# Expert stage of a mixture-of-experts block: the PE transposes of gathered rows replaced by a transposing DMA of 16-bit halves

## Chip, cores and metric

One NeuronCore of one Trainium2 chip runs the whole program in one launch. The metric is the device time of an execution in microseconds, lower is better.

## What is computed

The input x has 4096 rows of 256 float32. The block is `x += 0.5 * moe(norm(x))`, `x += attention(norm(x))`, `x += 0.5 * moe(norm(x))`. The mixture of experts, with 32 experts, 6 of them chosen for each row, is

```
scores = sigmoid(xf @ gate.T)                       # 4096 x 32
topk   = top_k(group-masked(scores + bias), 6)
tw     = 2.5 * scores[topk] / sum(scores[topk])
g, u   = xf @ gate_up[e][:128].T, xf @ gate_up[e][128:].T
routed = sum over chosen e of  tw_e * (silu(g) * u) @ down[e].T
out    = routed + shared expert(xf)
```

The attention part (a local one over segments of 64 rows and a global one over the segments' means) isn't touched by the change.

## The kernel before

The program runs six stages after one another: routing of the first mixture, its experts, the sum of the answers, attention with the routing of the second mixture beside it, the second mixture's experts, and the combining that writes the output.

**Routing.** For each pair of 128-row tiles, VectorE finds the six experts of every row, its six weights and six places. `act_route_rows` (L1227) copies the two normalised tiles on ScalarE (L1232, 128 partitions x 512 float32) into `rows`, whose rows are 320 floats long: 256 of data, 32 weights and 32 destinations, one for each expert. GpSimd scatters each row to its six places in the HBM tensor `dispatch_rows` by an indirect DMA (L632, L656).

**Experts.** The rows of an expert lie together in `dispatch_rows`, and are taken in blocks of 128: NB = 224 blocks for each of the two mixtures, so 448 turns in all. A table `itab` in SBUF holds each block's expert and first row; an engine's sequencer reads a number of it into a register (TENSOR_LOAD in the trace). A turn of block n is spread over the engines, each of which works through an order fixed by hand:

- SyncE (`sp_experts`): reads the block's first row from the table (L510) and issues the load of 128 x 320 floats into one of 4 buffers (L515).
- TensorE (`pe_experts`): transposes block n+2 into PSUM by two 128x128 products (`tx`, L831), multiplies block n by the staged gate and up weights (L711, 8 instructions of `xbt,ans`), and block n-2 by the down weights (L711, 2 instructions of `wdn,hb`).
- ScalarE (`act_experts`): silu of block n into `sg` (L1280), the copy of the gate and up weights of block n+2 from `wgu` into `staged` (L1274, recorded as `ans<-wgu`), the copy of the transposed block n+2 from PSUM to `xbt` (`xt_copy`, L1266), and the reading of one table entry, the expert of block n+3 (L1285).
- VectorE (`v_experts`): the product `hb` (L1714), the answer scaled by the row's weight (`yb`/`ans`, L1724), the scatter list `didx` (L1721), and two picks for each block (L1703): of the 32 weights and the 32 destinations in a row, the one that belongs to the block's expert.
- GpSimd (`pool_experts`): the indirect DMA that scatters the answers (L672), with 8 answer buffers.

TensorE waits for `staged` and `xt` of the block, ScalarE's silu waits for TensorE's `gu`, and the staging copy of block n+2 waits for `gu` of block n, whose buffer it takes.

Of the kernel before, what the change touches and what calls it, by code (L numbers as in the profile page):

```python
# [9 lines left out]
U32 = mybir.dt.uint32  # L10
ALU = mybir.AluOpType
# [26 lines left out]
COL_W, COL_DEST = D, D + E  # L38
# [71 lines left out]
def build(nc, x_in, gate_t, gate_bias, wgu_in, wdn_in, wsg_in, wsu_in, wsd_in,  # L110
          wi_l, bi_l, wo_l, bo_l, wi_g, bi_g, wo_g, bo_g, out):
    ctx = ExitStack()
    with ctx:
# [83 lines left out]
        rows = blk  # L197
        xbt = sb("xbt", [P, 2, D])
# [3 lines left out]
        picked = sb("picked", [P, 2, E])  # L202
        wcol = sb("wcol", [P, 8])
        dcol = sb("dcol", [P, 8])
        didx = sb("didx", [P, 8], I32)
# [40 lines left out]
        more_rows = flat[:, E * E + 4 * P:E * E + 4 * P + 4 * ROW].rearrange("p (q r) -> p q r", q=4)  # L246
        more_answers = flat[:, 0:4 * D].rearrange("p (q d) -> p q d", q=4)

        def block_rows(q):
            return blk[:, q, :] if q < 4 else more_rows[:, q - 4, :]  # L250
# [101 lines left out]
        LOADS, ANSWERS = 4, 8  # L352

        row_loads = [sem(f"ex_ld{q}") for q in range(LOADS)]

        class ExpertSems:
            def __init__(self, n):
# [5 lines left out]
                self.ld = row_loads  # L363
                self.loaded_by_now = n * 16 * (NB // LOADS)
                self.tx = s("ex_tx")
                self.xt = s("ex_xt")
# [132 lines left out]
        def sp_experts(sp, r, s):  # L499

            sp.wait_ge(s.tab, 1)
            for q in range(4):
                sp.wait_ge(r.scat[q], 16 * TOPK * (NT // 4))
            sp.wait_ge(padded, 16 * E)
            sp.wait_ge(ld_small, N_SMALL)

            def body(g, peeled):
                for q in range(LOADS):
                    n = g * LOADS + q
                    first = sp.value_load(itab[0:1, bass.ds(n + 2 * P, 1)], min_val=0, max_val=E * CAP - P)  # L510

                    if not peeled:
# [3 lines left out]
            body(0, True)  # L516
            with sp.Fori(1, NB // LOADS) as g:
                body(g, False)

        def sp_sum(sp, x, s):  # L520
            ans_v = answers_dram.rearrange("(n p k) d -> n p (k d)", p=P, k=TOPK)

            for q in range(ANSWERS):
                sp.wait_ge(x.scat[q], 16 * (NB // ANSWERS))
            for i in range(NT):
# [20 lines left out]
        def sp_combine(sp, x, s):  # L546
# [20 lines left out]
            for i in range(NT):  # L567
                load_answers(i)
                p = i // 2
                if i == 1:  # L570

                    sp.wait_ge(x.tx, NB)
                    sp.wait_ge(x.pick, 2 * NB)
# [42 lines left out]
        def pool_route_fours(pool, s):  # L616

            def pair(p, q0):
# [3 lines left out]
                for m in range(2 * TOPK):  # L623
# [4 lines left out]
                    if m == 8 and pair_exists(p + 1):  # L628
# [4 lines left out]
                        out=rows_dram, out_offset=bass.IndirectOffsetOnAxis(ap=idx[:, q, k:k + 1], axis=0),  # L633
                        in_=rows[:, q, :], in_offset=None).then_inc(s.scat[q], 16)
            pairs_by_two(pool, lambda p, k: pair(p, 2 * k), NT // 2)

        def pool_route_paced(pool, s):
# [5 lines left out]
            def pair(p, q0):  # L643
# [3 lines left out]
                for t in range(2):  # L647
                    i = p * 2 + (6 + t)
                    for k in range(TOPK):
                        if exists(i):  # L650
# [6 lines left out]
                            out=rows_dram, out_offset=bass.IndirectOffsetOnAxis(ap=idx[:, q, k:k + 1], axis=0),  # L657
                            in_=rows[:, q, :], in_offset=None).then_inc(s.scat[q], 16)
# [7 lines left out]
        def pool_experts(pool, s):  # L666
            with pool.Fori(0, NB // ANSWERS) as g:
                for q in range(ANSWERS):

                    pool.wait_ge(s.y, g * ANSWERS + (q + 1))  # L670
# [3 lines left out]
                        in_=block_answers(q), in_offset=None, bounds_check=T * TOPK - 1,  # L674
                        oob_is_err=False).then_inc(s.scat[q], 16)
# [136 lines left out]
        TX, GU, DN = 0, 2, 6  # L812
# [7 lines left out]
        def pe_experts(pe, s):  # L820
# [5 lines left out]
            def tx(n, q):  # L826

                b = q % LOADS
                pe.wait_ge(s.ld[b], loaded(s, n, b))
                for c in range(KC):  # L830
                    m = pe.transpose(ps[:, TX + q % 2, c * P:(c + 1) * P], block_rows(b)[:, c * P:(c + 1) * P], ident[:])  # L831
                m.then_inc(s.tx, 1)

            def step(n, q, m=None):
                j = q % 2
                if m is None or n < NB:
                    pe.wait_ge(s.staged, n + 1)
                    pe.wait_ge(s.xt, n + 1)  # L840

                    for half in range(2):
                        for c in range(KC):
                            g = mm(ps[:, GU + q % 4, half * P:(half + 1) * P],
                                   staged[:, j, c, half * I:(half + 1) * I],
                                   xbt[:, j, c * P:(c + 1) * P], start=(c == 0), stop=(c == KC - 1))
                    g.then_inc(s.gu, 1)
                if m is None or n >= 2:
                    e = pe.snap(expert[j], min_val=0, max_val=E - 1)
                    pe.wait_ge(s.h, n - 1)  # L850
                    positive(pe, s.y, n - 3)
                    mm(ps[:, DN + j, 0:D], hb[:, j, :], wdn[:, bass.ds(e * D, D)]).then_inc(s.d, 1)
                if m is None or n + 2 < NB:
                    tx(n + 2, (q + 2) % 8)
# [4 lines left out]
            tx(0, 0)  # L859
            tx(1, 1)  # L860
# [366 lines left out]
        def act_route_rows(act, s, p, k):  # L1227
# [4 lines left out]
            act.copy(rows[:, 2 * k:2 * k + 2, 0:D], xn[:, 2 * k:2 * k + 2, :]).then_inc(s.rx, 1)  # L1232
# [29 lines left out]
        def act_experts(act, s):  # L1262
            def xt_copy(n, j):
                act.wait_ge(s.tx, n + 1)
                positive(act, s.gu, n - 1)
                act.copy(xbt[:, j, :], ps[:, TX + j, 0:D]).then_inc(s.xt, 1)  # L1266

# [8 lines left out]
            def step(n, q, m=None):  # L1276
                j = q % 2
                act.wait_ge(s.gu, n + 1)
                positive(act, s.h, n - 1)
                act.activation(sg[:, j, :], ps[:, GU + q, 0:P], ACT.Silu).then_inc(s.sg, 1)  # L1280
# [6 lines left out]
            act.wait_ge(s.tab, 1)  # L1287
            act.wait_ge(ld_exp, 16 * 3 * (NT // 2))
            for j in range(2):
                act.reg_load(expert[j], itab[0:1, j:j + 1])  # L1290
            xt_copy(0, 0)
            stage(0, 0)
            xt_copy(1, 1)
            stage(1, 1)
            act.reg_load(expert[0], itab[0:1, 2:3])
            for n in range(4):
                step(n, n, m=0)
            with act.Fori(1, NB // 4 - 1) as g:
                for q in range(4):
                    step(g * 4 + q, q)  # L1300
            for n in range(NB - 4, NB):
                step(n, n % 4, m=0)
# [388 lines left out]
        def v_experts(v, st, s):  # L1691
            start = st.base + st.n
            st.rebase(start)

            def pick(n, q):

                b = q % LOADS
                v.wait_ge(s.ld[b], loaded(s, n, b))

                positive(v, s.pick, n * 2)  # L1700
                positive(v, s.y, n - 3)
                for k, (col, out_) in enumerate(((COL_W, wcol), (COL_DEST, dcol))):
                    v.scalar_tensor_tensor(  # L1703
                        out=picked[:, k, :], in0=iota_e[:], scalar=etab[:, bass.ds(n, 1)],
                        in1=block_rows(b)[:, col:col + E], op0=ALU.is_equal, op1=ALU.mult,
                        accum_out=out_[:, q:q + 1]).then_inc(s.pick, 1)

            def step(n, q, m=None):
# [6 lines left out]
                if m is None or n >= 2:  # L1715

                    at_, k = (q + 6) % 8, (q + 6) % 8 % ANSWERS
                    per = 16 // ANSWERS
                    positive(v, s.scat[k],
                             16 * ((n - 2) // ANSWERS) if isinstance(n, int) else n * per - (2 + k) * per)  # L1720
# [398 lines left out]
```

## Time and profile before

| | |
|---|---|
| time, median of 3 runs | 1511.45 us (1508.77 to 1520.38) |
| the profiled execution | span 1514.0 us; no separate device time is given for it |
| busy, of the span | PE 1311.2 (87%), DVE 1092.3 (72%), ACT 745.8 (49%), POOL 921.6 (61%) |
| DMA | 275.35 MB, mean 182 GB/s |

### The profile page before, as it was taken

The numbers are of one execution on the slowest core, as the hardware profiler recorded it, in microseconds if no ns is written. First come the engines' busy times: TensorE is split into PE (matmuls) and PEld (weight loads), VectorE is DVE, ScalarE is ACT, GpSimd is POOL, SyncE is SP. The second block draws the span as 40 slices with busy tenths as digits, with TensorE's granted clock in tenths as the row PEclk, the third lists the DMA queues.
The fourth block names the chain that finished last, engine by engine and source line by source line (L and its number), as shares of the span: only waits on it lengthen the run. The fifth ranks groups of instructions, "written<-read, shape, count | busy, mean of one in ns | idle before, by whom it ended". The sixth has DMA issues, their size and how long they took to land.

```text
span 1514.0 us, 50415 instructions
## 1 busy us (share of the span) xinstructions
PE 1311.2 (87%) x10768; PEld 1150.5 (76%) x10769; DVE 1092.3 (72%) x5484; ACT 745.8 (49%) x2296; POOL 921.6 (61%) x981
## 2 busy tenths in 40 slices
PE   6877772799999999789989998952999999999986
PEld 5766661699999999678766766742999999999765
DVE  6676654478888888576368888863788888888576
ACT  3433320466666666300356666721666666666100
POOL 3777777466666666422017776775566666666687
PEclk9776775899999999899699999955999999999998
DMA  9963333465556555397003333444565556564698
GB/s 316 404 248 130 126 130 127 146 184 184 186 185 190 181 187 178 119 330 256 1 29 136 142 131 131 147 174 144 176 188 187 184 183 186 180 184 139 231 315 280
DMA packets 155771, 275.35 MB, mean 182 GB/s; under 512 B 28966, under 2 KB 108091, under 8 KB 155712
## 3 DMA queue, kind: packets, MB, share of 16 engines
q1 hardware_dynamic: 115776, 161.32, 34.6%
q0 software_dynamic: 39936, 113.33, 20.2%
q8 instruction: 26, 0.43, 0.1%
q14 instruction: 33, 0.27, 0.1%
HBM read 147.64 MB, written 135.27 MB: 187 GB/s over the span
## 4 chain that ended last, share of the span: by engine, by line
PE 30%; DVE 7%; DMA 5%; issue 4%; POOL 3%; ACT 1%; DVEq 0%; SPq 0%; POOLq 0%; ACTq 0%
PE ps L711 26%; DMA ans<-answers 4%; PE ps L831 3%; POOL dispatch_rows L656 2%; DVE smax L1926 1%; DVE yb L1846 1%; POOL xres L693 1%; DVE stats L1469 0%; DVE prob L1936 0%; DVE rstd L1456 0%; DVE newt L1454 0%; DVE newt L1455 0%; PE ps L719 0%; DMA blk<-normed_transposed 0%; POOL answers L672 0%
## 5 line engine op out<-in xcount | busy, mean ns | idle before, releaser
L711 PE MATMUL ps<-xbt,ans 128*128 128x128 f32 x3584 | 477.0, 276 | 0.3 <-ACT ans L1274 0.3
L711 PEld LDWEIGHTS ps<-xbt,ans 128*128 128x128 f32 x3584 | 439.0, 193 | 0.9 <-ACT ans L1274 0.8
L672 POOL DMA_INDIRECT answers<-yb,didx x224 | 220.2, 983 | 160.9 <-issue 118.0
L672 POOL DMA_INDIRECT answers<-ans,didx x224 | 220.1, 983 | 122.2 <-issue 120.2
L1703 DVE SCALAR_TENSOR_TENSOR picked<-iota_e,etab,blk 128x32 f32<-128x32 f32 x896 | 190.7, 250 | 119.9 <-DVE yb L1724 40.1
L656 POOL DMA_INDIRECT dispatch_rows<-blk,idx x192 | 188.4, 981 | 142.9 <-issue 129.3
L1274 ACT COPY ans<-wgu 128x512 f32 x448 | 274.6, 613 | 0.2 <-issue 0.2
L711 PE MATMUL ps<-wdn,hb 128*128 x896 | 267.6, 381 | 1.3 <-DVE ans L1724 1.3
L632 POOL DMA_INDIRECT dispatch_rows<-blk,idx x192 | 187.3, 976 | 79.0 <-issue 57.2
L1280 ACT ACTIVATE sg<-ps 128x128 f32<-128x128 f32 x448 | 124.4, 278 | 218.5 <-PE ps L711 216.8
L831 PE MATMUL ps<-ident,blk 128*128 128x128 f32 x896 | 172.9, 275 | 33.6 <-DMA blk<-dispatch_rows 33.6
L1266 ACT COPY xbt<-ps 128x256 f32<-128x256 f32 x448 | 165.6, 370 | 64.6 <-PE ps L831 64.6
L831 PEld LDWEIGHTS ps<-ident,blk 128*128 128x128 f32 x896 | 126.9, 142 | 79.1 <-issue 33.0
L1714 DVE TENSOR_TENSOR hb<-ps,sg 128x128 f32<-128x128 f32 x448 | 130.6, 291 | 54.7 <-PE ps L711 23.6
L711 PEld LDWEIGHTS ps<-wdn,hb 128*128 128x128 f32 x896 | 136.0, 192 | 2.5 <-issue 2.5
L1724 DVE TENSOR_SCALAR ans<-ps,wcol 128x256 f32<-128x256 f32 x224 | 108.0, 482 | 1.1 <-PE ps L711 0.9
L1724 DVE TENSOR_SCALAR yb<-ps,wcol 128x256 f32<-128x256 f32 x224 | 108.3, 483 | 0.0
L1382 ACT ACTIVATE ans<-ps,nmax 128x64 f32<-128x64 f32 x256 | 76.4, 323 | 26.3 <-DVE nmax L1927 26.1
L711 PEld LDWEIGHTS ps<-xnt,wsgu 128*128 128x128 f32 x528 | 72.7, 216 | 2.8
L1703 DVE DVE_READ_ACCUMULATOR picked<-iota_e,etab,blk 128x1 f32 x896 | 74.5, 83 | 0.1
L711 PE MATMUL ps<-wsd,hsh 128*128 128x256 f32 x192 | 72.3, 543 | 2.2 <-DVE hsh L1832 2.2
L1721 DVE TENSOR_TENSOR didx<-dcol,ans 128x1 int32<-128x1 f32 x448 | 72.8, 163 | 0.0
(230 smaller groups left out, 1996.7 us busy)
## 6 DMA issues: line engine op xcount, KB each, us to landing
blk<-dispatch_rows SPq DMA_DIRECT2D x448, 160.0 KB
ans<-answers SPq DMA_DIRECT2D x54, 512.0 KB, 4.9
ans<-answers SPq DMA_DIRECT2D x54, 256.0 KB, 4.8
wgu<-in_gate_up SPq DMA_DIRECT2D x32, 256.0 KB
dispatch_rows<-blk,idx POOLq DMA_INDIRECT x384, 2.5
dispatch_rows<-padt SPq DMA_DIRECT2D x32, 160.0 KB
yb<-answers SPq DMA_DIRECT2D x10, 512.0 KB, 4.8
wdn<-in_down SPq DMA_DIRECT2D x16, 256.0 KB
```

Of the source, the lines that this page charges most:

```text
L632: pool.indirect_dma_start(out=rows_dram, out_offset=bass.IndirectOffsetOnAxis(ap=idx[:, q, k:k + 1], axis=0), in_=rows[:, q, :], in_offset ...
L656: pool.indirect_dma_start(out=rows_dram, out_offset=bass.IndirectOffsetOnAxis(ap=idx[:, q, k:k + 1], axis=0), in_=rows[:, q, :], in_offset ...
L672: pool.indirect_dma_start(out=answers_dram, out_offset=bass.IndirectOffsetOnAxis(ap=didx[:, q:q + 1], axis=0), in_=block_answers(q), in_of ...
L711: return nc.tensor.matmul(out_, lhs, rhs, start=start, stop=stop)
L831: m = pe.transpose(ps[:, TX + q % 2, c * P:(c + 1) * P], block_rows(b)[:, c * P:(c + 1) * P], ident[:])
L1266: act.copy(xbt[:, j, :], ps[:, TX + j, 0:D]).then_inc(s.xt, 1)
L1274: act.copy(staged[:, j, :, :], wgu[:, :, bass.ds(e * (2 * I), 2 * I)]).then_inc(s.staged, 1)
L1280: act.activation(sg[:, j, :], ps[:, GU + q, 0:P], ACT.Silu).then_inc(s.sg, 1)
L1382: a = act.activation(ssub[:, at_, :], ps[:, r, c * SEG:(c + 1) * SEG], ACT.Exp, bias=nmax[:, h:h + 1], scale=float(HDL) ** -0.5, accum_out ...
L1703: v.scalar_tensor_tensor(out=picked[:, k, :], in0=iota_e[:], scalar=etab[:, bass.ds(n, 1)], in1=block_rows(b)[:, col:col + E], op0=ALU.is_ ...
L1714: v.tensor_tensor(hb[:, j, :], ps[:, GU + q % 4, P:2 * P], sg[:, j, :], ALU.mult).then_inc(s.h, 1)
L1724: v.tensor_scalar(block_answers(k), ps[:, DN + j, 0:D], wcol[:, at_:at_ + 1], None, ALU.mult).then_inc(s.y, 1)
```

## The change

Rows are stored differently. In `dispatch_rows` a row of 320 floats becomes two planes of 320 16-bit numbers: the low (or high) halves of the 256 data values and half of the weights and destinations' space, then the other. `act_route_rows` writes this by a copy of 16-bit elements. For each block SyncE issues one transposing DMA, which sees the block as 256 rows (128 rows x 2 planes) of 256 16-bit numbers and writes them turned, so that SBUF holds float32 values, transposed; TensorE uses them as they land. TensorE's transposes and ScalarE's `xt_copy` are dropped. There are 8 such buffers in place of 4. The weights and destinations of a block (128 rows x 2 pieces of 128 bytes) are loaded by a second, plain DMA, which ScalarE issues at the end of the turn of the block eight before, after reading a second table entry. VectorE picks for four blocks at once, by one comparison, one product, one sum and one addition in four consecutive turns. TensorE's down product has four PSUM banks in place of two; the scatter lists have 16 columns in place of 8.

```diff
 # SyncE, for each block
-                    first = sp.value_load(itab[0:1, bass.ds(n + 2 * P, 1)], min_val=0, max_val=E * CAP - P)
-                        sp.wait_ge(s.tx, n - (LOADS - 1))
-                        sp.wait_ge(s.pick, n * 2 - (2 * LOADS - 2))
-                    sp.dma_start(block_rows(q), rows_dram[bass.ds(first, P), :]).then_inc(s.ld[q], 16)
+                    sp.reg_load(first[1 - q % 2], itab[0:1, bass.ds(n + 1 + 2 * P, 1)])
+                block_rows = rows_dram[bass.ds(at_, P), :]
+                positive(sp, s.gu, n - (LOADS - 1))
+                sp.dma_start_transpose(
+                    out=turned_halves(q % LOADS),
+                    in_=block_rows.bitcast(U16).rearrange("r (h x) -> (r h) x", h=2)[:, 0:D]
+                    ).then_inc(s.ld[q % LOADS], 16)
 # TensorE
-                    pe.wait_ge(s.xt, n + 1)
+                    pe.wait_ge(s.ld[q % LOADS], loaded(s, n, q % LOADS))
-                if m is None or n + 2 < NB:
-                    tx(n + 2, (q + 2) % 8)
 # ScalarE, routing
-            act.copy(rows[:, 2 * k:2 * k + 2, 0:D], xn[:, 2 * k:2 * k + 2, :]).then_inc(s.rx, 1)
+            act.copy(planes(rows[:, 2 * k:2 * k + 2, :])[:, :, :, 0:D],
+                     halves(xn[:, 2 * k:2 * k + 2, :])).then_inc(s.rx, 1)
 # ScalarE, experts
+            def load_pairs(n, q, group):
+                at_ = act.snap(first, min_val=0, max_val=E * CAP - P)
+                positive(act, s.pick, group - 1)
+                act.dma_start(pairs_of(q // PICKED % 2)[:, q % PICKED],
+                              rows_dram[bass.ds(at_, P), :].rearrange("r (h x) -> r h x", h=2)[:, :, D // 2:]
+                              ).then_inc(s.pairs[q // PICKED % 2], 16)
+                if not isinstance(n, int) or n + 1 < NB:
+                    act.reg_load(first, itab[0:1, bass.ds(n + 1 + 2 * P, 1)])
                 if m is None or n + 2 < NB:
                     stage(n + 2, j)
-                    xt_copy(n + 2, j)
                 if m is None or n + 3 < NB:
                     act.reg_load(expert[1 - j], itab[0:1, bass.ds(n + 3, 1)])
+                if m is None or n + 8 < NB:
+                    load_pairs(n + 8, q, n // PICKED + 2 if isinstance(n, int) else turn * 2 + q // PICKED + 2)
+            for n in range(8):
+                load_pairs(n, n, n // PICKED)
             act.wait_ge(ld_exp, 16 * 3 * (NT // 2))
 # VectorE, one of these in each turn, for four blocks
+            def mark(n):
+                st.did(v.tensor_tensor(
+                    mine, iota_e[:].unsqueeze(1).to_broadcast([P, PICKED, E]),
+                    etab[:, bass.ds(n, PICKED)].unsqueeze(2).to_broadcast([P, PICKED, E]), ALU.is_equal))
+            def take(k, paired):
+                v.wait_ge(s.pairs[k], paired)
+                v.tensor_tensor(picked, pairs_of(k), mine.unsqueeze(2).to_broadcast([P, PICKED, 2, E]),
+                                ALU.mult).then_inc(s.pick, 1)
+            def reduce_(k, group):
+                st.did(v.tensor_reduce(wd[:, k], picked, X_AXIS, ALU.add))
+            def lists(n, q):
+                st.did(v.tensor_tensor(didx[:, q:q + PICKED], wd[:, k, :, 1], skip[:, bass.ds(n, PICKED)], ALU.add))
```

## Rows read from the trace of the kernel before

**Rows 1.** Windows, one for each stage: busy us (instructions), granted clock, DMA share, GB/s

```profile
0.00:272.00 272.00, 177.86 (x940) 154.72 (x941) 165.26 (x874) 77.41 (x130) 189.53 (x213) 0.74 0.57 209
272.00:623.00 351.00, 347.94 (x2681) 324.83 (x2682) 277.32 (x1561) 237.80 (x671) 215.16 (x219) 0.99 0.58 177
...
1050.00:1403.00 353.00, 349.36 (x2689) 326.27 (x2690) 277.06 (x1567) 239.23 (x673) 215.61 (x220) 0.99 0.57 176
```

**Rows 2.** The chain that ended last: start us, us, what

```profile
1060.04 1.33 PE ps L711 x10
...
1381.57 1.33 PE ps L711 x10
```

**Rows 3.** Timeline of one turn: start us, us, what [idle before <- releaser]

```profile
552.28 0.60 PE L711 MATMUL ps<-wdn,hb 128*128 x2
552.48 0.28 ACT L1280 ACTIVATE sg<-ps 128x128 f32<-128x128 f32 x1 [0.40 <-PE ps L711]
...
552.65 0.61 ACT L1274 COPY ans<-wgu 128x512 f32 x1
...
552.71 0.38 PE L831 MATMUL ps<-ident,blk 128*128 128x128 f32 x2
...
552.93 1.06 PE L711 MATMUL ps<-xbt,ans 128*128 128x128 f32 x8
```

**Rows 4.** Sequencer instructions at three lines, 1060 to 1390 us: ns min/median/max

```profile
L1285 ACTq TENSOR_LOAD <-itab x214: 272/392/585, 1060.1 to 1389.4; - x107
L1285 ACTq FUSED_REGOPS  x212: 42/43/43, 1063.2 to 1389.3; - x106
...
L515 SPq DMA_DIRECT2D blk<-dispatch_rows x213: 332/333/408, 1061.4 to 1389.3; - x107
...
L510 SPq FUSED_REGOPS  x373: 46/152/159, 1060.4 to 1389.7; - x187
L510 SPq TENSOR_LOAD <-itab x214: 262/268/413, 1060.1 to 1389.8; - x107
```

**Rows 5.** Timeline of SyncE's queue: issues at the program's start and of the first blocks

```profile
1.30 0.50 SPq L448 DMA_DIRECT2D wgate<-in_gate  x1
...
4.91 8.75 SPq L459 DMA_DIRECT2D wil<-in_wi_local  x1
...
272.11 1.46 SPq L515 DMA_DIRECT2D blk<-dispatch_rows  x2
...
274.33 1.42 SPq L515 DMA_DIRECT2D blk<-dispatch_rows  x2
```

**Rows 6.** Timeline of the start of the first expert stage

```profile
275.30 0.62 ACT L1274 COPY ans<-wgu 128x512 f32 x1
```

**Rows 7.** Groups on DVE and ACT, 1060 to 1390 us: busy us, mean ns | idle before

```profile
L1703 DVE SCALAR_TENSOR_TENSOR picked<-iota_e,etab,blk 128x32 f32<-128x32 f32 x426 | 90.4, 250 | 45.0 <-DVE ans L1724 22.6 <-DVE yb L1724 20.2 <-issue 0.5
L1714 DVE TENSOR_TENSOR hb<-ps,sg 128x128 f32<-128x128 f32 x214 | 62.3, 291 | 20.5 <-PE ps L711 9.7 <-ACT sg L1280 0.3
L1724 DVE TENSOR_SCALAR yb<-ps,wcol 128x256 f32<-128x256 f32 x108 | 52.2, 483 | 0.0
...
L1266 ACT COPY xbt<-ps 128x256 f32<-128x256 f32 x214 | 79.1, 370 | 0.0
```

**Rows 8.** Timeline, GpSimd's shortest distances

```profile
67.34 0.96 POOL L632 DMA_INDIRECT dispatch_rows<-blk,idx  x1 [0.30 <-DVE yb L1484]
68.61 0.96 POOL L632 DMA_INDIRECT dispatch_rows<-blk,idx  x1 [0.30 <-issue]
...
1402.65 0.98 POOL L672 DMA_INDIRECT answers<-yb,didx  x1 [3.14 <-DVE ans L1724]
1403.94 0.98 POOL L672 DMA_INDIRECT answers<-ans,didx  x1 [0.30 <-DVE ans L1724]
```

**Rows 9.** The row copy, its line over the whole run: ns min/median/max

```profile
L1232 ACT COPY blk<-yb x32: 609/619/623, 11.8 to 1022.9; 128x512 f32<-128x512 f32 x32
```

**Rows 10.** DMA queues: packets, MB, share of 16 engines' span

```profile
q1 hardware_dynamic: 115776, 161.32, 34.6%
q0 software_dynamic: 39936, 113.33, 20.2%
```

**Rows 11.** Windows around a fall of the clock in the attention stage, columns as in rows 1

```profile
780.00:870.00 90.00, 81.73 (x1252) 62.63 (x1251) 75.94 (x361) 60.71 (x275) 58.01 (x60) 1.00 0.35 125
870.50:877.30 6.80, 5.24 (x102) 3.73 (x100) 5.73 (x26) 4.59 (x23) 4.61 (x6) 1.00 0.33 121
877.40:880.70 3.30, 3.30 (x8) 2.64 (x9) 2.52 (x13) 2.12 (x13) 2.39 (x4) 0.50 0.30 110
```

More of the change, by code:

```diff
@@ L10 @@
 U32 = mybir.dt.uint32
+U16 = mybir.dt.uint16
 ALU = mybir.AluOpType
@@ L197, in build, with planes, halves @@
         rows = blk
+        def planes(tiles):
+            return tiles.bitcast(U16).rearrange("p q (h x) -> p q h x", h=2)
+        def halves(tiles):
+            return tiles.bitcast(U16).rearrange("p q (d h) -> p q h d", h=2)
         xbt = sb("xbt", [P, 2, D])
@@ L349, in __init__ @@
                     self.sh_x = s("sh_x")
-        LOADS, ANSWERS = 4, 8
+        LOADS, ANSWERS, PICKED, LISTS = 8, 8, 4, 16
         row_loads = [sem(f"ex_ld{q}") for q in range(LOADS)]
+        pair_loads = [sem(f"ex_pairs{k}") for k in range(2)]
         class ExpertSems:
@@ L666, in pool_experts @@
         def pool_experts(pool, s):
-            with pool.Fori(0, NB // ANSWERS) as g:
-                for q in range(ANSWERS):
-                    pool.wait_ge(s.y, g * ANSWERS + (q + 1))
+            with pool.Fori(0, NB // LISTS) as g:
+                for q in range(LISTS):
+                    pool.wait_ge(s.y, g * LISTS + (q + 1))
                     pool.sem_inc(s.take, 1)
@@ L1260, in act_route, with act_experts @@
             pairs_by_two(act, body, NT // 2)
[L1262 to L1266, printed above, removed]
+        def act_experts(act, r, s):
             expert = [act.alloc_register(f"staged_expert{j}_{s.n}") for j in range(2)]
@@ L1290, in act_experts @@
                 act.reg_load(expert[j], itab[0:1, j:j + 1])
-            xt_copy(0, 0)
             stage(0, 0)
-            xt_copy(1, 1)
             stage(1, 1)
             act.reg_load(expert[0], itab[0:1, 2:3])
[L1296 to L1302, printed above, removed]
+            for n in range(8):
+                step(n, n, None, m=0)
+            with act.Fori(1, NB // 8 - 1) as g:
+                for q in range(8):
+                    step(g * 8 + q, q, g)
+            for n in range(NB - 8, NB):
+                step(n, n % 8, None, m=0)
         def act_combine(act, s):
@@ L1722, in step @@
-                    v.wait_ge(s.d, n - 1)
-                    v.wait_ge(s.pick, n * 2 - 2)
-                    v.tensor_scalar(block_answers(k), ps[:, DN + j, 0:D], wcol[:, at_:at_ + 1], None, ALU.mult).then_inc(s.y, 1)
-                    st.sync()
-                if m is None or n + 2 < NB:
-                    pick(n + 2, (q + 2) % 8)
-            pick(0, 0)
-            pick(1, 1)
-            for n in range(16):
-                step(n, n % 8, m=0)
-            with v.Fori(2, NB // 8 - 1) as g:
-                for q in range(8):
-                    st.rebase(g * 8 + (start + q - 2))
-                    step(g * 8 + q, q)
@@ L1737, in v_experts @@
-            st.rebase(start + NB - 8 - 2)
-            for n in range(NB - 8, NB + 2):
-                step(n, n % 8, m=0)
+                             16 * ((n - 2) // ANSWERS) if isinstance(n, int) else turn * 32 + 16 * ((q - 2) // ANSWERS))
+                    st.sync()
+                    v.tensor_scalar(block_answers(k), ps[:, DN + b % 4, 0:D], wd[:, b // PICKED % 2, b % PICKED, 0:1],
+                                    None, ALU.mult).then_inc(s.y, 1)
+                phase, group = q % PICKED, q // PICKED + 1
@@ new lines, in step @@
+                if m is None or n // PICKED * PICKED + PICKED < NB:
+                    if phase == 0:
+                        mark(n + PICKED)
+                    elif phase == 1:
+                        take(group % 2, s.paired_by_now + 64 * (group // 2 + 1) + (
+                            n // LISTS * 128 if isinstance(n, int) else turn * 128))
+                    elif phase == 2:
+                        reduce_(group % 2, n // PICKED + 1 if isinstance(n, int) else turn * 4 + group)
+                    else:
+                        lists(n + 1, (q + 1) % LISTS)
@@ new lines, in v_experts @@
+            mark(0)
+            take(0, s.paired_by_now + 64)
+            reduce_(0, 0)
+            lists(0, 0)
+            for n in range(LISTS):
+                step(n, n, None, m=0)
+            base_n = st.base + st.n
+            with v.Fori(1, NB // LISTS - 1) as g:
+                st.rebase(g * 12 + (base_n - 12))
+                for q in range(LISTS):
+                    step(g * LISTS + q, q, g)
+                assert st.n == 12, st.n
+            st.rebase(base_n + (NB // LISTS - 2) * 12)
@@ L1741, in v_sum @@
+            for n in range(NB - LISTS, NB + 2):
+                step(n, n % LISTS, None, m=0)
         def v_sum(v, st, s):
```

119 lines of the change are left out of this document (61 added, 58 removed).

## The prediction

> **What bounds the kernel.** I read the windows by stage first. In both expert stages TensorE is busy for all but 3 or 4 us (347.94 of 351.00, 349.36 of 353.00) at a granted clock of 0.99, that is the 2.4 GHz level, while ScalarE, VectorE and GpSimd stand at 238, 277 and 215 us [rows 1]. The chain of waits says the same in its own way: it runs through TensorE alone. Pieces of ten products (L711) of 1.33 us return from 1060.04 to 1381.57, which is 208 turns of 1.546 us [rows 2]; the 0.216 that is left of each turn is the two transposes (L831), and the timeline of a turn shows just that, 552.71 to 552.93 [rows 3]. So the stage is bound by TensorE's work, 448 turns of 1.546 us = 693 us of the 1514.0 us of the profiled execution. No device time of its own is given for that execution; its span is 2.6 us above the median 1511.45, and I add what changes to the median.
>
> **What TensorE gives up.** 448 x 0.216 = 97 us. That would be the gain if nothing else came late: 1.33 us a turn.
>
> **What ScalarE takes on.** Its busy time hides it. It gives up the 0.370 us copy (L1266) [rows 7], and the silu and the staging copy, 0.28 + 0.61, fill only 0.89 of a turn [rows 3]. But its sequencer works in order and carries out table reads and DMA issues itself, while its engine works off what was handed over. So I add up the sequencer's turn, from silu to silu, with 0.045 us between one sequencer instruction and the next. That distance I work out from SyncE: two issues span 1.46 or 1.42 us, so a turn of it is 1.09 to 1.12 [rows 5]; its durations are a table read 0.268, a check of 0.152, an issue of 0.333 [rows 4] and some 0.09 of small register operations (two like L1285's 0.043), 0.84 together, and the rest lies in six gaps.
> 1. Silu to staging copy: 0.17 (552.48 to 552.65) [rows 3]; then 0.05 to the next instruction.
> 2. Its own table read for the expert, already there today: 0.043 + 0.392 + two gaps = 0.52 [rows 4].
> 3. New, before the issue: a register move, a wait with its operand, the address; three times 0.035 to 0.045 plus gaps = 0.25.
> 4. New: the issue. SyncE's of one piece for each partition takes 0.333 [rows 4]; the load of `wgate`, 128 partitions x 2 pieces of 128 bytes and so of the very shape of the new one, took 0.50 [rows 5]. With gap 0.38 to 0.55. ScalarE issues no DMA before, so both are SyncE's prices. I take the lower, since the issues of one-piece loads at the program's start were dearer than those in the stage, too.
> 5. New: the second table read, 0.043 + 0.392 + two gaps = 0.52.
> 6. The two waits ahead of the next silu: 0.14; the step over the loop's end, shared by eight turns, 0.03 at most.
>
> The sum is 0.22 + 0.52 + 0.25 + 0.38 + 0.52 + 0.14 = 2.03; part of the small operations overlap with the gaps in my count, and the table reads vary from 0.272 to 0.585 [rows 4], so with reads of 0.272 it is 1.79. The low end, with gaps of 0.035 as well, is 1.72; the high end, with 0.50 for the issue, is 2.16. I take 1.96, nearer the row of the median read than that of the shortest. None of it waits for TensorE, so nothing hides it once TensorE's own turn is 1.33: silu of n+1 and the staging of n+3 queue behind it, and TensorE waits for `staged`. What covered ScalarE until now was its wait of 0.40 for TensorE in each turn [rows 3]; the cover is smaller than what is added (1.15 us added, about 0.15 given up with `xt_copy`). Turns with the new load: 432 of 448 (the last eight of each stage have none and gain 0.21 each). 432 x (1.96 - 1.546) = +179, less 3 = **+176 us**.
>
> The Trainium skill, "DMA: Bandwidth & Descriptors", section "Issuing engines are not separate DMA queues", says that starting DMAs from several engines saves only the sequencer's time for initiating them, which is usually small beside the DMA. By that rule the new issue would cost nothing, and it points to the first rival below. The rows of this case speak against "small": 0.333 to 0.50 us in a turn of 1.546.
>
> **The start of each expert stage.** ScalarE now issues eight loads before its first staging copy, and waits for the last scatter first. It starts where SyncE starts, at 272.1 [rows 5]. Eight times SyncE's turn without its check, 0.93, or with the dearer issue and reads 1.2, is 7.4 to 9.6; two reads follow, 0.8. The first staging copy moves from 275.30 [rows 6] to about 281.5. Nothing hides it, TensorE has no other work. Twice +6 = **+12 us**. The transposed blocks land in that time.
>
> **The row copy.** L1232 takes 0.619 us for 512 elements [rows 9]. With 16-bit halves there are 1024. From 256 elements at 0.370 [rows 7] to 512 at 0.619 each costs 0.97 ns, so it takes 1.12, +0.50 for each of 32 pairs. In the first routing GpSimd sets the pace (189.53 us busy in scatters 1.27 apart [rows 1, 8]), and the copy is done a pair ahead: nothing. In the attention stage 16 of them are beside busy engines; between 0 and 8 us, I take **+5**. If 16-bit elements went faster it would be at most 0.6 x 16 = 10 less; nothing here shows that.
>
> **VectorE.** It gives up two picks (2 x 0.25 and more than 0.1 behind them) and a list of 0.16 in each turn, and does one of four: a comparison of 128 elements, at most 0.29 like `hb`, a product of 256 and a sum of 256, 0.48 each like the answer [rows 7], an addition. With `hb` and the answer a turn is at most 0.29 + 0.48 + 0.48 = 1.25 us, below 1.33. It ends nothing.
>
> **GpSimd.** Its shortest distances are 1.27 and 1.29 us [rows 8]: below 1.33. It is 0.04 from being the next bound, and free here.
>
> **SyncE.** It no longer has the check, but a DMA whose kind no row shows: read, operations and gaps come to 0.6, so at a turn of 1.96 the issue may take 1.3 us unnoticed, at 1.33 only 0.7. From below: a plain issue, 0.333. From above: an issue held by a full queue took 8.75 [rows 5]. I take it as hidden, nearest to the plain issue by size (128 KB against 160).
>
> Sum: 1511.45 + 176 + 12 + 5 = **1705 us**. Its own range, from turns of 1.72 to 2.16 us, is 1600 to 1795. Chance 0.53.
>
> **Rivals.**
>
> *TensorE stays the bound (faster).* If the issue is handed on at once and the second read overlaps, ScalarE's turn falls below 1.33 and the stage runs at TensorE's pace: 1511.45 - 97 + 12 + 5 = about 1432, with GpSimd's 1.29 right behind. For it: ScalarE's engine is idle a third of the turn. Against it: on SyncE issue, read and next issue follow one another without overlap. It decides if the sequencer's turn is under 1.33, against my 1.72 at the least. Chance 0.17. In between, a turn of 1.48 to 1.54, lies no change: 0.06.
>
> *The transposing DMA sets the pace (slower still).* Packets of SyncE's queue take 0.346 x 16 x 1514 / 115776 = 72 ns, those of GpSimd's 0.202 x 16 x 1514 / 39936 = 123 ns [rows 10]. A turn loads 128 and scatters some 32 now: 0.58 + 0.25 us of 16 engines. If the 256 half rows go as 256 packets at 72 ns the turn needs 1.15 + 0.25 + up to 1.15 for the small pieces; as 512 packets, 2.3 + 0.25 and more, some 2.6. It decides from 1.96 on, and at 2.6 gives 1511 + 448 x 1.05 + 17 = 2000. Chance 0.15. The Trainium skill has two figures, in sentences that the sum does without. "DMA: Bandwidth & Descriptors", section "Latency and other measured facts", gives a transposing DMA 261 GB/s: an estimate of 0.50 us for 131 KB, no bound. "VectorE: DVE Perf Modes", section "The three transpose paths", gives 1309 ns for 128 x 128 in 16 bits; a block is four of them, by an estimate 5.2 us if they followed one another, and the time would be over 3000. No row here shows either.
>
> *TensorE's clock falls.* With 1.33 us of work in 1.96, TensorE has a gap in every turn. In the attention stage the clock stayed at 1.00 with TensorE busy for 81.73 of 90.00 us, and fell to 0.50 (1.2 GHz) after a stretch with 5.24 of 6.80, which is 77%; 3.4 us later it was back [rows 11]. At that level a turn's work takes 2.66. If 3.4 of every 10.2 us went so, they would hold 3.4/2.66 + 6.8/1.96 = 4.75 blocks, 2.15 us for one: +82, 1787 us. Chance 0.09.
>
> **From cases to numbers.** Faster by over 1%: the first rival, 0.17. Within 1%, about what a measurement of this kernel can tell from no change: 0.06. Slower by over 1%: 0.53 + 0.15 + 0.09 = 0.77. To leave out no more than 2 in 10 the range must reach from the faster rival to above the clock's: 1430 to 1850; the likeliest case's own range is 1600 to 1795.
>
> **What the changed profile would show.** If I am right: ScalarE's sequencer without waits in the stage, silu to silu in 1.7 to 2.15 us, TensorE idle before its L711 for `staged` (the copy `ans<-wgu`), its busy share in the stage near 70 to 80%, the first staging copy some 6 us later. If TensorE's gaps end with the landing of the turned rows, it is the transposing DMA; if granted clock is 0.5 in stretches, the third rival; if L711 pieces follow at 1.33, the first. The prediction fails above all if ScalarE's issue or reads cost half of what I assume.

## The result and the profile after

The changed kernel takes 1737.21 us, median of 4 runs (1733.9 to 1743.72), against 1510.92 for the kernel before; the ratio is 1.1502, interval 1.1471 to 1.1533. The prediction was 1705, with 1600 to 1795 for its likeliest case.

The windows of the profiled execution (span 1742.0 us), cut at the same events as in [rows 1]:

```profile
0.00:270.20 270.20, 175.49 (x940) 151.93 (x941) 165.57 (x875) 84.20 (x130) 189.26 (x213) 0.72 0.58 210
270.20:735.00 464.80, 357.43 (x2248) 270.96 (x2248) 206.52 (x677) 178.56 (x452) 218.36 (x222) 0.98 0.61 133
...
1169.00:1630.00 461.00, 357.56 (x2251) 271.22 (x2252) 205.26 (x671) 178.07 (x449) 216.86 (x221) 0.98 0.61 135
```

Nearly all of the loss lies in the two expert stages: 925.8 us against 704, of a span that grew by 228. TensorE was busy for 99% of them before; now it is for 77%, and no other engine is busier: by busy time nobody bounds the stage. The chain of waits of the page names what busy time leaves out:

```profile
PE 14%; ACTq 12%; issue 8%; DVE 5%; ACT 5%; DMA 4%; POOL 2%; DVEq 0%; SPq 0%; POOLq 0%
PE ps L738 13%; ACTq L1293 5%; ACTq L1297 4%; ACT ans L1286 3%; DMA ans<-answers 3%; ACTq L1307 2%; POOL dispatch_rows L683 1%; DMA blk<-normed_transposed 1%; DVE smax L1973 1%; DMA dispatch_rows<-blk,idx 1%; DVE yb L1893 1%; ACT ans L1393 0%; ACTq L1286 0%; DVE stats L1497 0%; ACT sg L1303 0%
```

ACTq is ScalarE's sequencer: the issue of the small load (L1293), the read of its first row (L1297), the read of the expert (L1307). Before, ACTq stood at 0%. The waits from 300 to 700 us say who waits in consequence (engine, line <- releaser: us in total, times, longest):

```profile
DVE hb L1750 <- ACT sg L1303: 191.1, 168, 1.9
...
ACT sg L1303 <- PE ps L738: 113.4, 79, 1.8
...
PE ps L738 <- ACT ans L1286: 89.2, 195, 1.0
```

TensorE waits for the staging copy once in each of some 200 turns, and not once in this list for the turned rows. The middle line says that the silu waited for TensorE 79 times. That is only the event that came last before the silu; what ScalarE did meanwhile is read from its sequencer, below.

The turn itself, from the line of the silu (first and last start of each stage):

```profile
L1303 ACT ACTIVATE sg<-ps x224: 271/277/278, 282.2 to 729.3; 128x128 f32<-128x128 f32 x112
...
L1303 ACT ACTIVATE sg<-ps x224: 269/277/279, 1181.2 to 1626.3; 128x128 f32<-128x128 f32 x112
```

(729.3 - 282.2)/223 = 2.005 us and 1.996 us, against 1.546 of [rows 2]. What fills it, by the sequencers' lines, 300 to 700 us (ns min/median/max):

```profile
L1297 ACTq TENSOR_LOAD <-itab x196: 274/382/780, 300.0 to 698.7; - x196
...
L1307 ACTq TENSOR_LOAD <-itab x196: 271/278/312, 300.8 to 699.4; - x196
...
L1293 ACTq DMA_DIRECT2D blk<-dispatch_rows x98: 550/551/588, 301.3 to 695.8; - x98
...
L534 SPq DMA_TRANSPOSE blk<-dispatch_rows x100: 1186/1189/1362, 299.9 to 693.3; - x100
...
L530 SPq TENSOR_LOAD <-itab x198: 263/329/607, 301.2 to 698.7; - x198
```

ScalarE: 0.28 + 0.38 for the reads, 0.55 for the issue, the rest small operations and gaps. But SyncE has a long turn too: the transposing issue holds its sequencer for 1.19 us (the plain issue of [rows 4] 0.33), and with a read of 0.33 and the rest a turn of SyncE's own would be some 1.8 to 1.9.

The lines above don't tell two engines with turns so near each other apart. The distances between one sequencer instruction and the next, added up, do; between two that don't wait it is 0.03 to 0.05 us. From 300 to 700 us ScalarE's sequencer stands still for more than 0.13 us only 25 times, 5.6 us in all, of which 5.3 lie at the end of its loop: it doesn't wait, whatever the list of waits names. SyncE's stands still 82 times, 25.8 us in all, each time ahead of an issue, where it waits for a buffer to come free. So SyncE follows, with 0.13 us of slack in a turn. The experiments test this.

### The profile page after: what moved, and what is told of

Same layout as the page of the kernel before. It is cut to its first block, busy times and chain, and to the rows that moved or that the text cites. A ratio compares the mean times of both kernels' runs of the same rounds, so it can differ in the third digit from the quotient of the medians.

```text
span 1742.0 us, 44022 instructions
## 1 busy us (share of the span) xinstructions
PE 1332.0 (76%) x9872; PEld 1041.7 (60%) x9873; DVE 948.2 (54%) x3692; ACT 636.6 (37%) x1848; POOL 923.2 (53%) x981
## 3 DMA queue, kind: packets, MB, share of 16 engines
q1 hardware_dynamic: 294976, 146.67, 31.0%
## 4 chain that ended last, share of the span: by engine, by line
PE 14%; ACTq 12%; issue 8%; DVE 5%; ACT 5%; DMA 4%; POOL 2%; DVEq 0%; SPq 0%; POOLq 0%
PE ps L738 13%; ACTq L1293 5%; ACTq L1297 4%; ACT ans L1286 3%; DMA ans<-answers 3%; ACTq L1307 2%; POOL dispatch_rows L683 1%; DMA blk<-normed_transposed 1%; DVE smax L1973 1%; DMA dispatch_rows<-blk,idx 1%; DVE yb L1893 1%; ACT ans L1393 0%; ACTq L1286 0%; DVE stats L1497 0%; ACT sg L1303 0%
## 5 line engine op out<-in xcount | busy, mean ns | idle before, releaser
L738 PE MATMUL ps<-blk,ans 128*128 128x128 f32 x1792 | 261.1, 290 | 149.2 <-ACT ans L1286 149.0
L738 PEld LDWEIGHTS ps<-blk,ans 128*128 128x128 f32 x1792 | 220.9, 194 | 234.8 <-issue 230.5
L738 PE MATMUL ps<-kt,ans 128*128 128x128 f32 x896 | 128.8, 287 | 44.2 <-ACT ans L1286 44.1
L738 PE MATMUL ps<-prob,ans 128*128 128x128 f32 x896 | 128.6, 286 | 43.1 <-ACT ans L1286 42.9
L738 PEld LDWEIGHTS ps<-kt,ans 128*128 128x128 f32 x896 | 108.7, 191 | 87.1 <-issue 84.1
L738 PEld LDWEIGHTS ps<-prob,ans 128*128 128x128 f32 x896 | 108.9, 191 | 85.4 <-issue 84.1
L1758 DVE TENSOR_SCALAR ans<-ps,wd 128x256 f32<-128x256 f32 x224 | 106.3, 476 | 0.3 <-PE ps L738 0.2
L1758 DVE TENSOR_SCALAR yb<-ps,wd 128x256 f32<-128x256 f32 x224 | 106.3, 474 | 0.0
L738 PE MATMUL ps<-xnt,wsgu 128*128 128x128 f32 (+1 forms) x528 | 68.8, 292 | 0.0
L746 PE MATMUL ps<-ident,yb 128*128 128x128 f32 x128 | 30.6, 328 | 42.2 <-DVE yb L1512 38.7
```

What stands on the lines that cost most here:

```text
L738: return nc.tensor.matmul(out_, lhs, rhs, start=start, stop=stop)
L1758: v.tensor_scalar(block_answers(k), ps[:, DN + b % 4, 0:D], wd[:, b // PICKED % 2, b % PICKED, 0:1], None, ALU.mult).then_inc(s.y, 1)
```

## Experiments

Theory 1: ScalarE's sequencer sets the turn of 2.00. Theory 2: SyncE's transposing issue does. Theory 3: the DMA engines or the landing do.

On two of the chips used, the kernel before itself took 1909 and 1881 us. ScalarE and VectorE stop there now and then for several us, for up to 20.3 in the routing, and the profile names nothing of this program as the releaser ("remote"). Kernels whose sequencers were relieved (below) still had turns of 2.10 and 2.05 us on them, so something else sets the pace there. I call these chips disturbed, and compare each run only with kernels on a chip of the same kind.

### Twice the same read: an edit that wasn't there

```diff
+                    act.reg_load(first, itab[0:1, bass.ds(n + 1 + 2 * P, 1)])   # ScalarE, doubled
+                    sp.reg_load(first[1 - q % 2], itab[0:1, bass.ds(n + 1 + 2 * P, 1)])   # SyncE, in the other kernel
```

> The changed kernel with the second table read of ScalarE's turn (the first row for the small load) done twice; results are the same. Theory 1, ScalarE's sequencer sets the turn of 2.00 us: every turn grows by a read and its address, 0.35 to 0.50 us, so +150 to +215 on 1737, about 1910. Theory 2, SyncE's transposing issue (1.19 us, with its read and waits some 1.9) sets it and ScalarE has only followed: ScalarE's slack would take most of it, under +60. Theory 3, the DMA engines or the landing of the turned rows set it: no change.

> The changed kernel with SyncE's table read done twice; results are the same. Theory 1: SyncE's own turn is 1.85 to 1.93 us against ScalarE's 2.00, so of the 0.35 to 0.40 us added some 0.1 is hidden: a turn of 2.2 to 2.3, +100 to +130. Theory 2: nothing is hidden, +155 to +180. Theory 3: under +20, since buffers are loaded eight blocks ahead.

> The same kernel as act_extra_read, beside a kernel before of some 1515. If ScalarE's sequencer sets the turn of 2.00 us (theory 1), each of its turns grows by 0.35 to 0.50: a turn of 2.35 to 2.5, 1890 to 1960. If SyncE at 1.82 to 1.93 set it with ScalarE only following (theory 2), ScalarE at its own 1.85 to 2.0 plus the read would still pass it, but by less: under +100 on 1737. If the DMA engines set it (theory 3), no change.

Measured: 1895.85 and 1895.76 us on a chip where the kernel before takes 1908.95 (ratios 0.989 and 0.994); the third, on an ordinary chip, 1739.88 against 1511.73, ratio 1.150 [1.145, 1.156], as the changed kernel. The pages show why: all three runs have 44022 instructions, exactly as many as the changed kernel. The doubled read isn't in any of the three; since its result is overwritten by the next, it was most likely dropped as dead. So these say nothing on any theory; they are three more runs of the changed kernel. They give two useful things: its time repeats, and on a chip of the disturbed kind it takes 1896 with a turn of (813.6 - 364.8)/223 = 2.01.

### A read that is used

```diff
-                act.copy(staged[:, j, :, :], wgu[:, :, bass.ds(e * (2 * I), 2 * I)])
+                act.copy(staged[:, j, :, :], wgu[:, :, bass.ds(e * I + e2 * I, 2 * I)])
+                    act.reg_load(again[1 - j], itab[0:1, bass.ds(n + 3, 1)])
```

> The changed kernel with a third table read in ScalarE's turn, of the block's expert again into another register, and both registers in the staging copy's address, so that no read can be dropped as dead (act_extra_read had as many instructions, 44022, as the changed kernel: its doubled read wasn't there). Results are the same. ScalarE's sequencer as the bound: 0.28 to 0.45 for the read, 0.1 to 0.15 for its operations, a turn of 2.4 to 2.6, so 1910 to 2010. If ScalarE had slack: under +50 on 1737.

Measured: 2021.64 us on a disturbed chip (the kernel before: 1881.22; ratio 1.0762 [1.0711, 1.0812]), where the changed kernel had 1895.85 on the other of that kind. The new read and the silu:

```profile
L1310 ACTq TENSOR_LOAD <-itab x171: 274/276/574, 400.3 to 797.9; - x171
```

```profile
L1305 ACT ACTIVATE sg<-ps x224: 277/278/278, 356.7 to 872.3; 128x128 f32<-128x128 f32 x112
```

The turn is (872.3 - 356.7)/223 = 2.31, 0.30 more than 2.01; 448 x 0.30 = 134, and the times differ by 126. Both are under what I expected of theory 1 (a turn of 2.4 to 2.6, 173 to 273 us more) and over the 50 us that slack would have left. The new read takes 0.276 us, and its gap and operations come on top, but the read of the first row became shorter at the same time, from a median of 0.377 us in act_extra_read to 0.280. The two chips aren't the same one, which is this run's weak point; its own trace makes up for it. From 400 to 800 us ScalarE's sequencer stands still for over 0.13 us for 5.4 us in all, nearly all of it at the end of its loop, and SyncE's for 94.2. So the turn of 2.31 is what ScalarE's sequencer needs. That is theory 1.

### SyncE relieved

A plain load of the same bytes takes the place of the transposing one, so the experts' inputs aren't transposed, and the routing's row copy moves 512 float32.

```diff
-                sp.dma_start_transpose(
-                    out=turned_halves(q % LOADS),
-                    in_=block_rows.bitcast(U16).rearrange("r (h x) -> (r h) x", h=2)[:, 0:D]
+                sp.dma_start(
+                    turned_rows(q % LOADS).rearrange("p (h x) -> p h x", h=2),
+                    block_rows.rearrange("r (h x) -> r h x", h=2)[:, :, 0:D // 2]
```

> SyncE issues a plain load of the same 128 KB (two pieces of 512 bytes a row) in place of the transposing DMA, and the row copy of the routing moves 512 float32 in place of 1024 16-bit halves. The experts' inputs then aren't transposed, all other work is done. SyncE's issue should fall from 1.19 to about 0.5 us. Theory 1: ScalarE's sequencer still sets the turn, 1.8 to 2.0, so 1650 to 1730; if its reads were lengthened by SyncE's issues, it is the lower end. Theory 2 and 3: the turn falls to TensorE's 1.33 to 1.5, 1440 to 1510. The attention stage with the routing shows what the dearer row copy costs: 0 to 14 us less than in the changed kernel.

> The same kernel as plain_in_place_of_transposing (experts' inputs not transposed, a plain load of the same bytes, a row copy of 512 float32), beside a kernel before of some 1515. Theory 1: ScalarE alone holds the turn at 1.8 to 2.0, 1640 to 1735. Theory 2 or 3: SyncE or the DMA engines are relieved and the turn falls toward 1.33 to 1.5. In the attention stage the cheaper row copy gives back 0 to 14 us.

Measured: 1896.23 on the disturbed chip (before: 1908.95, ratio 0.992), which can't tell them apart; on an ordinary one 1718.83 against 1511.73, ratio 1.137 [1.132, 1.142].

```profile
L1303 ACT ACTIVATE sg<-ps x224: 270/277/279, 283.3 to 726.2; 128x128 f32<-128x128 f32 x112
```

```profile
L534 SPq DMA_DIRECT2D blk<-dispatch_rows x98: 542/543/544, 299.7 to 690.6; - x98
```

SyncE's issue fell from 1.19 to 0.54 us, and the turn from 2.00 to (726.2 - 283.3)/223 = 1.99. SyncE's sequencer now stands still for 162.2 us of 400, ScalarE's for 5.6 as before. Theories 2 and 3 fall: neither SyncE nor the transposing in the DMA engines held the turn of the changed kernel. Against act_extra_read_2 on the same chip the time fell by 21 us: some 7 are the turns, and 10 lie between the two expert stages, where two profiles of the changed kernel differ by as much (see the row copy, below).

### ScalarE relieved

One table read in every eighth turn fills eight registers.

```diff
-                    act.reg_load(expert[1 - j], itab[0:1, bass.ds(n + 3, 1)])
-                    act.reg_load(first, itab[0:1, bass.ds(n + 1 + 2 * P, 1)])
+                    if q == 6:
+                        act.reg_load(expert, itab[0:1, bass.ds(n + 2, 8)])
+                    if q == 0:
+                        act.reg_load(first, itab[0:1, bass.ds(n + 8 + 2 * P, 8)])
```

> ScalarE reads eight experts and eight first rows by one table read each in every eighth turn, into eight registers, in place of two reads in each turn; results are the same. Theory 1: ScalarE's turn falls by 0.28 + 0.41 + operations, some 0.75, to 1.3, and SyncE becomes the bound at 1.85 to 1.93: 1670 to 1705. Theory 2: the same end, so only by how little it gains do they differ (theory 2: nothing). Theory 3: no change. If neither SyncE nor DMA held it, TensorE's 1.33 would give about 1440.

> The same kernel as scalar_reads_batched, again, since in that call the kernel before itself took 1909 us and every variant landed beside it: scatters there paused for 3 to 4 us at a time, also in the routing. Beside a kernel before of some 1510: theory 1 (ScalarE's sequencer sets the turn of 2.00 us) expects ScalarE's own turn to fall to about 1.1 and SyncE's, 1.85 to 1.93, to take over: 1670 to 1705. Theory 2 (SyncE's transposing issue set it all along): under 20 us gained. Theory 3 (DMA engines or landing): no change.

Measured: first 1923.83 on the disturbed chip (before: 1908.95, ratio 1.008), with a turn of (832.0 - 364.7)/223 = 2.10, no answer; then 1656.46 against 1517.25, ratio 1.0929 [1.0885, 1.0972]. The turn is (687.6 - 282.1)/223 = 1.82:

```profile
L1302 ACT ACTIVATE sg<-ps x224: 277/278/278, 282.1 to 687.6; 128x128 f32<-128x128 f32 x112
```

and TensorE's weight loads now wait for another:

```profile
ACT sg L1302 <- PE ps L738: 190.0, 199, 2.3
...
PEld ps L738 <- DMA blk<-dispatch_rows: 70.1, 89, 2.0
```

Taking two reads of ScalarE's away gave 81 us; adding one cost 126. The difference between removing and adding is SyncE, which stood 0.18 us behind ScalarE and became the bound: its sequencer doesn't once stand still for over 0.13 us from 300 to 680 us, while ScalarE's does for 117 us. The time is below my 1670 to 1705, since SyncE's read takes a median of 0.268 us now and took 0.329 in the changed kernel.

### Both relieved, with and without the transposing

```diff
-                    sp.reg_load(first[1 - q % 2], itab[0:1, bass.ds(n + 1 + 2 * P, 1)])
+                if q % 8 == 0:
+                    sp.reg_load(first, itab[0:1, bass.ds(n + 2 * P, 8)])
```

> As before, and SyncE too reads eight first rows at once in every eighth turn; results are the same. SyncE's turn becomes the issue of 1.19 us, some 0.2 of operations and gaps, and an eighth of a read of 0.55: 1.45 to 1.5. Theories 1 and 2 both expect that turn, so 1480 to 1530, near the kernel before; if theory 3 holds (the turned rows cost the DMA engines more than the issue shows) it stays above 1600. TensorE's own 1.33 is not reached.

> Plain load in place of the transposing DMA (experts' inputs not transposed) and both engines' table reads batched by eight. ScalarE's turn is 1.1, SyncE's 0.8, so TensorE at 1.33 or GpSimd at 1.29 to 1.33 sets it: 1511 - 97 + 10 = 1420 to 1440, the price of the prediction's first rival. If it stays above 1480, the DMA engines (by 16-bit halves or by small pieces) or a wait that no theory has are the bound.

Measured: with the transposing DMA 1534.22 against 1517.25, ratio 1.0127 [1.0084, 1.017], just above my 1480 to 1530; with the plain load 1449.86 against 1511.73, ratio 0.9563 [0.9505, 0.962], above my 1420 to 1440. Silu lines and the windows 300 to 570 us, with transposing:

```profile
L1301 ACT ACTIVATE sg<-ps x224: 277/278/278, 282.2 to 630.6; 128x128 f32<-128x128 f32 x112
```

```profile
300.00:570.00 270.00, 247.88 (x1712) 209.31 (x1711) 157.59 (x513) 136.63 (x342) 169.24 (x173) 1.00 0.91 181
```

and with the plain load:

```profile
L1301 ACT ACTIVATE sg<-ps x224: 277/277/279, 280.3 to 588.2; 128x128 f32<-128x128 f32 x112
```

```profile
300.00:570.00 270.00, 268.51 (x1955) 244.62 (x1955) 178.79 (x585) 156.09 (x390) 192.92 (x196) 1.00 0.79 207
```

Turns of 1.56 and 1.38 us. Plain, TensorE is busy for 268.51 of 270 again: the rival that the prediction priced at 1432 exists, once both sequencers are out of the way, and costs 1450. With the transposing issue it can't be reached. The DMA engines are busy for 0.91 of the stage, against 0.79 plain at a faster turn, so both they and SyncE could hold the last 0.18 us. TensorE waits for the turned rows in this kernel:

```profile
PEld ps L737 <- DMA blk<-dispatch_rows: 32.4, 47, 1.4
```

SyncE's sequencer is the nearer cause: from 300 to 600 us it stands still for over 0.13 us for 7.7 us in all, 4.5 of them at the end of its loop, so it hardly waits for a free buffer and issues as fast as it can. What fills its turn of 1.56 is the issue, 1.22 us in the mean, an eighth of a table read of eight (below), and small operations with their gaps:

```profile
L529 SPq TENSOR_LOAD <-itab x23: 521/543/808, 310.4 to 589.8; - x23
```

The DMA engines' part is at most that the issue grows longer as they are busier: its mean is 1.19 us at a share of 0.53 (the kernel with the used read), 1.20 at 0.63, 1.22 at 0.91. Why it does isn't shown.

### Toward a version that beats both

```diff
+            stage(0, 0)
+            stage(1, 1)                       # ScalarE: now ahead of the wait for the last scatter
             for q in range(4):
                 act.wait_ge(r.scat[q], 16 * TOPK * (NT // 4))
-                    sp.reg_load(first, itab[0:1, bass.ds(n + 2 * P, 8)])
+                    sp.reg_load(first, itab[0:1, bass.ds(n + 2 * P, 16)])
```

> On both_reads_batched (1534): ScalarE stages its first two weights before it waits for the last scatter and issues its eight loads, and SyncE reads 16 first rows at once in a loop of 16 blocks; results are the same. The first takes 3 to 5 us from each stage's start, the second some 1.0 us from every 16 turns, 14 a stage: -28 us if SyncE sets the turn. 1495 to 1515 if so; if the DMA engines, busy for 0.89 of the stage there, set it, 1520 to 1530.

> On early_staging_reads_of_16 (1522.6), SyncE reads 32 first rows at once in a loop of 32 blocks; results are the same. If SyncE's sequencer sets the turn, some 1.0 us less from every 32 turns, so -10 to -14: 1508 to 1513, the time of the kernel before. If the DMA engines set it, busy for 0.93 of the stage there: no gain, 1518 to 1525.

Measured: with 16, 1522.6 against 1511.73, ratio 1.0046 [1.0016, 1.0077], a turn of (621.7 - 278.2)/223 = 1.54 with the DMA engines at 0.93; with 32, 1879.87 against 1881.22 on a disturbed chip, ratio 0.9979 [0.9955, 1.0004], which doesn't tell whether 32 gains over 16.

The 1522.6 falls into the range that I had put down to the DMA engines, but the trace doesn't say so: SyncE's sequencer never stands still for over 0.13 us from 300 to 600 us. I had priced the gain wrongly. A read of 16 costs nearly what two of eight do, where I had expected 1.0 us from every 16 turns, and the mean issue rose from 1.22 to 1.24 us:

```profile
L529 SPq TENSOR_LOAD <-itab x12: 837/1102/1192, 320.5 to 593.4; - x12
```

No transposing version beats the kernel before. The silu of the first block starts at 278.2, against 282.2: that is the cost of the eight issues ahead of the staging copy.

## Why the prediction was right

**TensorE's work and the gain it would give.** Right that a gain waited behind the sequencers, but 97 us isn't what the runs show of it: the plain kernel with batched reads had a turn of 1.38 and not 1.33, as its ten products for a block fill 1.37 us (268.51 us for 1955 products). That is 0.166 us less than 1.546, or 74 us in 448 turns, and the time was 62 us less than before.

**ScalarE's sequencer.** The step that decided, and right as a mechanism: predicted 1.96 us, measured 2.00. Its trace shows no waits, as the prediction said it would, and three runs carry it: with a used read the turn grows and ScalarE's sequencer stays full, relieving SyncE changes the turn by 0.01, relieving ScalarE lowers it to SyncE's.

How near the number came is in part luck, since mis-sized terms cancelled. The issue takes 0.551 us, where I took 0.333 and named 0.50 from the row of `wgate` as the upper price: the load of the same shape, not the nearest in time, was the right row. ScalarE's own read, carried over at 0.392, takes 0.278 now; the new one has 0.382. Together +0.22, -0.11 and -0.01 make +0.10 us on the sum of 2.03. The turn came out 0.03 below that sum, so its small operations and gaps were 0.13 too dear. That I took 1.96 and not the sum of 2.03 was a judgement for the shorter reads, and no run shows it as such. By its own terms the high end of the turn was 2.20 (2.03 - 0.333 + 0.50) and not 2.16; the measured 2.00 is inside both.

Why the one read takes 0.28 us and the other 0.38 isn't shown. The dearer one coincides with a table read of TensorE's (L875) in 195 of 196 turns, the cheaper one never; but in the kernel with the used read 21 that coincide have a median of 0.279.

The Trainium skill says that issuing is usually small beside the DMA ("DMA: Bandwidth & Descriptors", section "Issuing engines are not separate DMA queues"). In plain_in_place_of_transposing_2 the small load of 32 KB lands a median of 2.4 us after its issue, so 0.551 us is about a quarter of it. What decided here is another comparison: 0.551 us of a turn of 2.00.

The 0.04 us by which 1.96 was missed are, over 432 turns, 17 us of the 32 by which the time was; in the profile the stages' turns cost 448 x 0.455 = 204 us, where I had 176.

**The start of each stage.** Predicted +6 each. From ScalarE's first issue at 270.26 to its first staging copy at 279.26 it is 9.0 us, against 3.2 before (272.11 to 275.30): +5.8. The stage began 1.9 us earlier than before, so the first silu came 4.1 us later (282.2 against 278.1), and this is what staging early gave back.

```profile
270.26 3.80 ACTq L1293 DMA_DIRECT2D blk<-dispatch_rows  x4
270.62 6.47 SPq L534 DMA_TRANSPOSE blk<-dispatch_rows  x4
274.55 3.64 ACTq L1293 DMA_DIRECT2D vv<-dispatch_rows  x4
...
279.26 1.14 ACT L1286 COPY ans<-wgu 128x512 f32 x2 [39.65 <-issue]
```

**The row copy.** Predicted 1.12 us, measured:

```profile
L1248 ACT COPY blk<-yb x32: 1036/1045/1049, 11.8 to 1141.4; 128x1024 uint16<-128x1024 uint16 x32
```

Its price in the time isn't settled. From the last silu of the first expert stage to ScalarE's first small load of the second it is 440.1 and 429.7 us in two profiles of the changed kernel (after, act_extra_read_2), 428.7, 429.2 and 439.9 in three other kernels with this copy, 419.3 and 427.6 in two with the float32 copy, all on ordinary chips, and 426.5 before, up to SyncE's first load. My +5 lies within that spread.

**VectorE and GpSimd.** Right that neither ends anything: 179 and 193 busy of 400 us in the row below.

**SyncE.** I allowed its issue 1.3 us unnoticed at a turn of 1.96 and took it as nearest to a plain issue. It is 1.19: far from the plain 0.33, and just inside the allowance. Had ScalarE been free, as in my first rival, this alone would have kept the turn at 1.8 (1.82 with ScalarE's reads batched), so that rival had less than its 0.17; it needed two conditions and I had named one.

**The transposing in the DMA engines.** It didn't set the pace, but it isn't free: 0.63 of the stage at a turn of 2.00, so 1.26 us a turn where the old kernel had 0.58 x 1.546 = 0.90. I had priced its packets at 72 ns. There are more and shorter ones:

```profile
q1 hardware_dynamic: 294976, 146.67, 31.0%
...
q10 hardware_dynamic: 121856, 14.71, 6.2%
```

0.310 x 16 x 1742 / 294976 = 29 ns each. Before, the queue had 115776 - 448 x 128 = 58432 packets beside the block loads, which gives (294976 - 58432)/448 = 528 for a turned block: my second rival had their number about right, and failed by their price. Of the two figures cited from the Trainium skill, the 1309 ns of "VectorE: DVE Perf Modes", section "The three transpose paths", can't be the pace at which four for each block follow one another, since a whole turn took 1.56 us with both sequencers relieved; how long a single block takes to land no view shows. The estimate of 0.50 us for 131 KB from "DMA: Bandwidth & Descriptors", section "Latency and other measured facts", is neither shown nor contradicted.

**TensorE's clock.** It didn't fall, though TensorE is busy for 78% of the stage, as in the stretch of [rows 11] before a fall:

```profile
300.00:700.00 400.00, 310.59 (x1958) 232.94 (x1956) 179.15 (x587) 154.60 (x392) 192.55 (x196) 1.00 0.63 141
```

What tells the two apart isn't shown; here TensorE's waits for `staged` are 1.0 us at most and come once in each turn.
